# Attention scores by head in 32-row tiles, moved SBUF to SBUF into (column, head) rows, then mixed as one fp32 matmul a row pair; the low halves of the attention output on GpSimd

## The chip, the cores and the metric

The kernel runs on one core of one Trainium2 chip. The metric is the device time of one execution in microseconds (us). A core has five engines with a queue of instructions each: TensorE (PE, matmuls; PEld is its weight load), VectorE (DVE), ScalarE (ACT), GpSimd (POOL) and SyncE (SP, which here only issues DMAs). They run beside each other and wait for one another by semaphores. SBUF is the memory of 128 partitions that the engines read and write; PSUM holds the results of matmuls in 8 banks, which this kernel uses in four pairs: `psA`, `psL`, `psM`, `psC`.

## The reference

The input is 128 images of 384 channels and 14 x 14 = 196 pixels. After a group norm, a block of eight-head attention is added to it:

```python
q = conv1x1_bn(x, qw, ...)   # 8 heads x 32 channels, 196 pixels
k = conv1x1_bn(x, kw, ...)   # the same
v4 = conv1x1_bn(x, vw, ...)  # 8 heads x 128 channels
vl = depthwise 3x3 conv of v4, scaled and shifted
attn = jnp.einsum('bhid,bhjd->bhij', q, k) * SCALE
attn = attn + ab[:, BIAS_IDXS][None]
attn = jnp.einsum('bhij,gh->bgij', attn, th1w) + _c(th1b)
attn = jax.nn.softmax(attn, axis=-1)
attn = jnp.einsum('bhij,gh->bgij', attn, th2w) + _c(th2b)
o = jnp.einsum('bhij,bhjd->bhid', attn, v)
o = relu(o in channels first + vl)
return conv1x1_bn(o, pw, ...)    # x + this is the output
```

The heads are mixed twice: by `th1w` before the softmax and by `th2w` behind it.

## The kernel before

It works through 64 pairs of images, one pair in a round (`step(t, first, last)` on each engine; round 0 and the last one are written apart, the 62 between them are a loop). The order on each engine is the order in which its code is written; waits on counting semaphores tie the engines together.

A matmul of 32-bit data comes in two kinds here. A plain fp32 matmul is run by the chip as two instructions over the columns. The fp32r kind takes one instruction, but keeps fewer bits, so a product is made of three of them (`split3`, L293): high half by low half, low by high, high by high. The halves are made by a cast (ACT) and a subtraction.

TensorE's order in a round is this. Twelve projection tiles of 9 fp32r matmuls with 392 columns each (`qkv_tile`, both images side by side): value tiles 0 and 1, four tiles of queries and keys, value tiles 2 to 7. Then two of the three tiles of the output projection of the pair before (`project`, 24 matmuls each). Then the logits, already mixed by `th1w`: for each of 14 steps, two image rows `b` of queries (14 pixels by 8 mixed heads are 112 rows) by 196 keys, as 12 fp32r matmuls of 196 columns, since the mixing weight is multiplied into the queries, and all 8 heads' 256 channels are summed. The third projection tile follows; then 14 uses of the second mixing (`L404`, which also turns the attention into rows by key, against `mixw`); then `attn` by values (`L426`), eight units of one image and two heads (4 fp32 matmuls each, 196 columns).

The operands of the logits cost the other engines work: 16 scaled copies `q_hi` on ACT (`mixed_high`, L486), 16 `q_lo` on DVE (`mixed_low`, L722), two `k_hi` on ACT (L490), two `k_lo` on POOL (L857). DVE also does the depthwise convolution, 64 instructions a round (`conv`, L700), two block transposes of the values (L730), for each logit row the bias and the row's maximum (L759), the sum of attention and convolution (`s_add`, L794) and the low half `o_lo` of the relu's output (`low`, L787). ACT takes projection results out of PSUM, makes the exponentials (L584, 28 rows), copies the mixed attention out of PSUM (L601), puts the values into head order (`head_major`, L494) and applies the relu (`o_hi`, L461). POOL normalises the next pair (L822), makes `mixw` (L844), adds the residual (L833) and makes `x_lo` of the next pair (L827), for which TensorE's next round waits (`s_xlo`).

SP issues, in a round: the next pair's input; 8 DMAs of the transposed values to DRAM (L254); a row of ones; 4 DMAs that bring them back by key (L267); the store of the pair before; the residual's load.

## Time and profile before

| | |
|---|---|
| median of 3 runs | 4534.61 us (4534.28 to 4535.59) |
| profiled execution, its own time | 4534.58 us |
| its span, first to last instruction | 4532.8 us |
| granted TensorE clock over the span | 0.999 |
| busy: PE, DVE, ACT, POOL | 4505.5, 4197.4, 3570.3, 1360.9 us |
| share of PE in the chain that ended last | 99% |

The page divides the span by engine, by stretch of time and by group of instructions. The busy time of a group is the union of its instructions. The mean of one is longer than the distance between two starts, because an engine overlaps the end of one instruction with the next: a 392-column fp32r matmul has a mean of 341 to 345 ns, while 156 of them in a row take 27.85 us, 0.1785 us each. The distances are what fills an engine's time, so those are read from the timeline and from the chain in order of time.

### The profile page before, as it was taken

To read this page: it belongs to the slowest core of one execution; us is meant where nothing else is said; L and a number is where in the kernel's file an instruction comes from. 1 tells how busy PE (TensorE), PEld (TensorE's weight loads), DVE (VectorE), ACT (ScalarE), POOL (GpSimd) and SP (SyncE) were. 2 spreads that over 40 slices of the span, in tenths; PEclk is the share of its full clock that TensorE was granted. 3 is DMA by queue.
4 is the path that set the end of the run, shared out by engine and by line. 5 is a ranking of instruction groups with operands and counts; after the bars stand their busy time and mean duration, and the time that the engine had idled before them with its cause. 6 is when DMAs were issued, how large, how long until landed. Compare 5 with 4: busy or idle time off the path is not lost.

```text
span 4532.8 us, 108461 instructions
## 1 busy us (share of the span) xinstructions
PE 4505.5 (99%) x33666; PEld 4502.5 (99%) x33666; DVE 4197.4 (93%) x10015; ACT 3570.3 (79%) x8508; POOL 1360.9 (30%) x1288
## 2 busy tenths in 40 slices
PE   7999999999999999999999999999999999999999
PEld 7999999999999999999999999999999999999999
DVE  8999999999999999999999999999999999999998
ACT  7787877878778787787787877878778778787786
POOL 2323323323233232332322323323233232332322
PEclk9999999999999999999999999999999999999999
DMA  3322222223222232222322322223222232232222
GB/s 94 97 65 81 86 69 87 65 81 92 70 81 74 72 97 65 81 82 68 93 65 81 88 72 82 68 78 97 65 81 79 67 97 65 81 86 68 88 65 76
DMA packets 211502, 356.05 MB, mean 79 GB/s; under 512 B 15843, under 2 KB 132691, under 8 KB 211413
## 3 DMA queue, kind: packets, MB, share of 16 engines
q1 hardware_dynamic: 211478, 355.75, 27.3%
q8 instruction: 13, 0.21, 0.0%
q14 instruction: 11, 0.09, 0.0%
HBM read 199.71 MB, written 155.98 MB: 78 GB/s over the span
## 4 chain that ended last, share of the span: by engine, by line
PE 99%; DMA 0%; POOL 0%; DVE 0%; SPq 0%; ACT 0%; issue 0%; POOLq 0%; DVEq 0%
PE psA L293 45%; PE psA L426 15%; PE psL L293 13%; PE psM L293 10%; PE psM L404 9%; PE psL L404 7%; PE psA L306 0%; DMA qa<-in_wqkv 0%; SPq L254 0%; POOL xs L822 0%; DVE probs L730 0%; DMA by_key<-probs 0%; POOL wp_lo L863 0%; DVE q_lo L722 0%; ACT w_hi L443 0%
## 5 line engine op out<-in xcount | busy, mean ns | idle before, releaser
L700 DVE SCALAR_TENSOR_TENSOR psC<-vpad,par,psC 128x406 f32<-128x406 f32 x3072 | 1807.2, 635 | 0.0
L584 ACT ACTIVATE probs<-probs,nmax 112x196 f32<-112x196 f32 x1792 | 803.2, 451 | 128.8 <-DVE nmax L759 112.9
L293 PE MATMUL psA<-x_hi,w_lo 128*128 128x392 f32 x2304 | 794.9, 345 | 6.0 <-DVE x_lo L679 6.0
L293 PE MATMUL psA<-x_hi,w_hi 128*128 128x392 f32 x2304 | 785.7, 341 | 0.0
L293 PE MATMUL psA<-x_lo,w_hi 128*128 128x392 f32 x2304 | 785.1, 341 | 0.0
L426 PE MATMUL psA<-qa,shared 105*128 105x196 f32 x4096 | 690.9, 329 | 0.0
L426 PEld LDWEIGHTS psA<-qa,shared 105*128 105x128 f32 x4096 | 677.2, 190 | 0.4 <-DVE shared L794 0.3
L857 POOL TENSOR_TENSOR k_lo<-qk,k_hi 128x392 fp32r<-128x392 f32 x128 | 159.9, 1249 | 1636.4 <-ACT k_hi L490 1636.4
L722 DVE SCALAR_TENSOR_TENSOR q_lo<-qk,th,q_hi 128x392 fp32r<-128x392 f32 x1024 | 618.3, 632 | 2.0 <-ACT q_hi L486 1.9
L486 ACT ACTIVATE q_hi<-qk,th 128x392 fp32r<-128x392 f32 x1024 | 594.5, 618 | 2.1
L461 ACT ACTIVATE o_hi<-shared 128x392 fp32r<-128x392 f32 x512 | 271.6, 530 | 391.3 <-DVE shared L794 391.3
L293 PE MATMUL psL<-k_hi,q_lo 128*112 128x196 f32 x2048 | 534.4, 261 | 5.3 <-DVE q_lo L722 4.2
L293 PE MATMUL psL<-k_lo,q_hi 128*112 128x196 f32 x2048 | 536.2, 262 | 0.0
L293 PE MATMUL psL<-k_hi,q_hi 128*112 128x196 f32 x2048 | 535.9, 262 | 0.0
L293 PE MATMUL psA<-o_hi,wp_lo 128*128 128x392 f32 x1536 | 526.6, 343 | 0.0
L293 PE MATMUL psA<-o_lo,wp_hi 128*128 128x392 f32 x1536 | 523.1, 341 | 0.0
L293 PE MATMUL psA<-o_hi,wp_hi 128*128 128x392 f32 x1536 | 521.0, 339 | 0.0
L844 POOL TENSOR_TENSOR mixw<-kron,rinv 112x448 f32<-112x448 f32 (+1 forms) x512 | 455.9, 921 | 135.5 <-DVE rinv L773 123.3
L510 ACT ACTIVATE vpad<-psA,par 128x392 f32<-128x392 f32 x512 | 349.5, 683 | 141.6 <-PE psA L293 135.0
L700 DVE SCALAR_TENSOR_TENSOR psC<-vpad,par,shared 128x406 f32<-128x406 f32 x512 | 327.4, 661 | 143.0 <-ACT shared L456 143.0
L293 PEld LDWEIGHTS psA<-x_hi,w_lo 128*128 128x128 f32 x2304 | 434.3, 189 | 6.4 <-issue 6.4
L404 PE MATMUL psM<-mixw,probs 113*105 113x112 f32 x4096 | 435.9, 260 | 4.6 <-POOL mixw L844 4.6
(85 smaller groups left out, 10723.1 us busy)
## 6 DMA issues: line engine op xcount, KB each, us to landing
by_key<-probs SPq DMA_DIRECT2D x512, 224.0 KB, 3.6
qa<-by_key SPq DMA_DIRECT2D x128, 448.0 KB, 4.3
qk<-by_key SPq DMA_DIRECT2D x128, 448.0 KB, 6.9
xs<-in_x SPq DMA_DIRECT2D x64, 588.0 KB, 3.8
shared<-in_x SPq DMA_DIRECT2D x64, 588.0 KB, 3.8
out<-shared SPq DMA_DIRECT2D x63, 588.0 KB, 3.0
qa<-in_wqkv SPq DMA_DIRECT2D x3, 768.0 KB, 7.1
stage_wp<-in_wp SPq DMA_DIRECT2D x1, 1536.0 KB, 9.6
```

The costliest lines, as they stand in the source:

```text
L293: last = nc.tensor.matmul(dst, w, r, start=(begin and n == 0), stop=(end and n == 2))
L404: mm = nc.tensor.matmul(bank[:, jc, :, b, :], probs[0:HP + 1, img, 2 * n + b, jc * HALF:(jc + 1) * HALF], mixw[0:HP + 1, img, 2 * n + b, : ...
L426: mm = nc.tensor.matmul(psA[:, u % 2, e * PIX:(e + 1) * PIX], vt[0:HALF, img, jc, g * D:(g + 1) * D], attn[:, img, jc, g, :], start=(jc == ...
L461: nc.scalar.activation(o_hi[:, 2 * n:2 * n + 2, img * PIX:(img + 1) * PIX], acc[:, 2 * n:2 * n + 2, img * IMG:img * IMG + PIX], ACT.Relu). ...
L486: nc.scalar.activation(q_hi[dst], src, ACT.Copy, scale=th1[:, kt, g:g + 1]).then_inc(s_qhi, 1)
L510: nc.scalar.activation(dst[:, :, 0:RES, 0:RES], psA[:, m % 2, 0:COLS].rearrange("p (i r w) -> p i r w", i=2, w=RES), ACT.Identity, bias=qk ...
L584: nc.scalar.activation(row, row, ACT.Exp, bias=nmax[:, img, b:b + 1], scale=-1.0, accum_out=rowsum[:, img, b:b + 1]).then_inc(s_exp, 1)
L700: nc.vector.scalar_tensor_tensor(a if tap == 7 else sums, src, taps[:, c, TAPS[tap]:TAPS[tap] + 1], a if tap == 0 else sums, MUL, ADD).the ...
L722: nc.vector.scalar_tensor_tensor(q_lo[dst], src, th1[:, kt, g:g + 1], q_hi[dst].bitcast(f32), MUL, SUB).then_inc(s_qlo, 1)
L844: nc.gpsimd.tensor_tensor(mixw[0:HP, img, b0:b0 + nb, :], k2, rinv[:, img, b0:b0 + nb].unsqueeze(2).broadcast_to([HP, nb, HP]), MUL).then_ ...
L857: nc.gpsimd.tensor_tensor(k_lo[:, kt, :], k[:, kt, :], k_hi[:, kt, :].bitcast(f32), SUB).then_inc(s_klo, 1)
```

## The change

Scores are now made by head, before any mixing. `head_scores` comes behind each of value tiles 2 to 5: for one image and one part of the query pixels (8 of 14 columns `w`, or the other 6), 8 plain fp32 matmuls of 32 channels (one head) by 196 keys; four heads lie on four groups of 32 partitions and write four different PSUM banks. ACT and DVE copy the result to `scores` (two copies each). SP then moves each head's block with one DMA from `scores` (rows by query pixel) to `by_head`, whose row is (column `w`, head), with the image row `b` and the key along it: 8 DMAs a unit, 32 a round. Each has 112 or 84 runs of 784 bytes, and writes 8 or 6 partitions. The first mixing is now one plain fp32 matmul of 392 columns for each of the 14 steps, with `kron1` as weights. `q_hi`, `q_lo`, `k_hi` and `k_lo` are gone.

Around that: the three projection tiles of the pair before stand behind mixing matmuls 3, 7 and 11; the values are transposed by image, behind rows 3 and 7, and their way through DRAM follows the moves on SP's queue; the row of ones is loaded once; the units of `attn` by values go head pair by head pair with the two images in turn, and wait for all 14 copies of the mixed attention; ACT applies the relu twice (to `o_hi` and in place), POOL makes `o_lo` from the two (`low`); `x_high` of the next pair stands behind the first relu, and `x_low` behind POOL's first `low`; POOL takes over the head order of image 0's values.

```diff
+        heads_at = VT // 2 * ACC
+        by_head = shared[0:HP, heads_at:heads_at + 2 * RES * PIX].rearrange("p (i n) -> p i n", i=2)
...
+            def moves(t, u):
+                img, c = UNITS[u]
+                sp.wait_ge(s_score_a, 8 * t + 2 * u + 2)
+                sp.wait_ge(s_score_v, 8 * t + 2 * u + 2)
+                lo, hi = c * WIDE // RES, (c * WIDE + score_rows(c)) // RES
+                for h in range(NH):
+                    sp.dma_start(by_head[lo * NH + h:(hi - 1) * NH + h + 1:NH, img, :].rearrange("w (b j) -> w b j", b=RES),
+                                 scores[0:score_rows(c), img, c, h, :]).then_inc(s_moved[u], 16)
...
+            def head_scores(t, first, u):
+                img, c = UNITS[u]
+                if u:
+                    pe.wait_ge(s_score_a, 8 * t + 2 * u)
+                    pe.wait_ge(s_score_v, 8 * t + 2 * u)
...
+                at_ = img * PIX + c * WIDE
+                for kt in range(QT):
+                    for r in range(QUADS):
+                        part_ = slice(r * KD, (r + 1) * KD)
+                        mm = nc.tensor.matmul(score_bank(r)[0:score_rows(c), kt * PIX:(kt + 1) * PIX],
+                                              q[part_, kt, at_:at_ + score_rows(c)],
+                                              k[part_, kt, img * PIX:(img + 1) * PIX], start=True, stop=True)
+                mm.then_inc(s_score_mm, 1)
...
+                    if n % 7 == 0:
+                        pe.wait_ge(s_moved[2 * img], MOVES * (t + 1))
+                        pe.wait_ge(s_moved[2 * img + 1], MOVES * (t + 1))
...
-                            mm = split3(logit_bank(n)[:, (b - b0) * PIX:(b - b0 + 1) * PIX],
-                                        q_lo[:, img * RES + b, kt, :], q_hi[:, img * RES + b, kt, :],
-                                        k_lo[:, kt, px], k_hi[:, kt, px], kt == 0, kt == QT - 1)
-                    mm.then_inc(s_logit_mm, 1)
+                    nc.tensor.matmul(logit_bank(n)[:, 0:2 * PIX], kron1[:, :, :].rearrange("p g i -> p (g i)"),
+                                     by_head[:, img, b0 * PIX:(b0 + 2) * PIX], start=True, stop=True
+                                     ).then_inc(s_logit_mm, 1)
...
+                pe.wait_ge(s_mix_sb, 14 * t + 14)
+                for u in range(8):
+                    n, img = divmod(u, 2)
...
+                nc.scalar.activation(o_hi[:, 2 * n:2 * n + 2, img * PIX:(img + 1) * PIX], a, ACT.Relu).then_inc(s_relu, 1)
+                nc.scalar.activation(a, a, ACT.Relu).then_inc(s_relu, 1)
...
+                convs(13)
+                if first:
+                    dve.wait_ge(s_wlo, CT)
+                for u in range(4):
+                    score_copies(u)
+                    convs(2 if u < 3 else 3)
...
+                    if n in (3, 7):
+                        turn(n // 4)
+                        convs(2)
+                    if n == 11:
+                        convs(5)
...
-                convs(3)
-                convs(64)
+                convs(22)
...
+                nc.gpsimd.tensor_tensor(o_lo[sl], a, o_hi[sl].bitcast(f32), SUB).then_inc(s_olo, 1)
...
                 mixing_weights(t, first, 0)
+                head_major(t, 0)
+                head_major(t, 1)
                 mixing_weights(t, first, 1)
                 if not first:
                     residual(t, 2)
+                low(t, first, 0)
```

On TensorE in the loop, behind value tile 2 (`psA` is the projections' pair of banks), there stood before the next projection tile at once:

```order
L293 MATMUL psA<-x_hi,w_hi 128x392
L359 REGISTER_ALU
L293 MATMUL psA<-x_hi,w_lo 128x392 [waits s_qk_sb]
L293 MATMUL psA<-x_lo,w_hi 128x392
L293 MATMUL psA<-x_hi,w_hi 128x392
```

Now the first unit of scores stands between the two tiles (`qk_room` holds queries and keys):

```order
L309 MATMUL psA<-x_hi,w_hi 128x392
L358 REGISTER_ALU
L360 REGISTER_ALU [waits s_qk_sb]
L365 MATMUL psL<-qk_room 112x196 [waits s_mix_sb]
L365 MATMUL psL<-qk_room 112x196
L365 MATMUL psM<-qk_room 112x196 x2
L365 MATMUL psL<-qk_room 112x196 x2
L365 MATMUL psM<-qk_room 112x196 x2
L309 MATMUL psA<-x_hi,w_lo 128x392 [waits s_qk_sb]
```

Eight matmuls of the scores have come in between two tiles, four heads and then the other four.

On TensorE where the logits begin, there stood before, behind two whole projection tiles (`o_hi,wp_hi` is the last of them):

```order
L293 MATMUL psA<-o_hi,wp_hi 128x392
L369 REGISTER_ALU
L370 REGISTER_ALU [waits s_klo]
L376 ISA [waits s_qlo]
L293 MATMUL psL<-k_hi,q_lo 112x196 [waits s_mix_sb]
L293 MATMUL psL<-k_lo,q_hi 112x196
L293 MATMUL psL<-k_hi,q_hi 112x196
```

Now the first mixing matmuls stand directly behind the last value tile (`shared` holds `by_head`, `kron` is `kron1`), and the first projection tile behind the fourth of them:

```order
L309 MATMUL psA<-x_hi,w_hi 128x392
L406 REGISTER_ALU
L409 REGISTER_ALU [waits s_score_v,s_score_a]
L413 MATMUL psL<-shared,kron 112x392 [waits s_moved1,s_moved0]
L413 MATMUL psL<-shared,kron 112x392
L413 MATMUL psM<-shared,kron 112x392
L417 REGISTER_ALU
L418 REGISTER_ALU [waits s_v_sb]
L322 MATMUL psA<-mv,same 128x4 [waits s_stat]
L413 MATMUL psM<-shared,kron 112x392
```

The 48 projection matmuls that lay between the last value tile and the logits are gone from there, three logit steps of 12 matmuls each are three single ones, and the first of them waits for the DMAs of units 0 and 1.

On SP in the loop, behind the load of the next pair's input, there stood before:

```order
L225 DMA xs<-in_x 128x2x588
L251 ISA
L254 DMA by_key<-probs 32x7x256 [waits s_turned]
L254 DMA by_key<-probs 32x7x256 x7
L259 REGISTER_ALU
L260 DMA probs<-in_ones 1x3584 [waits s_vt_out]
L264 REGISTER_ALU
L267 DMA qa<-by_key 112x1024 [waits s_logit_mm]
```

Now 32 moves come first (`qa` holds `scores`, and later `turned`):

```order
L227 DMA xs<-in_x 128x2x588
L286 REGISTER_ALU
L261 REGISTER_ALU [waits s_olo,s_av_mm]
L265 DMA shared<-qa 8x14x196 [waits s_score_v,s_score_a]
L265 DMA shared<-qa 8x14x196 x7
L261 REGISTER_ALU
L265 DMA shared<-qa 6x14x196 [waits s_score_v,s_score_a]
L265 DMA shared<-qa 6x14x196 x7
L261 REGISTER_ALU
L265 DMA shared<-qa 8x14x196 [waits s_score_v,s_score_a]
L265 DMA shared<-qa 8x14x196 x7
L261 REGISTER_ALU
```

The transposed values' way out to DRAM stands behind all four units on this queue, and has the same 8 DMAs, four an image.

## Rows read from the trace of the kernel before

**Rows 1.** Page: the chain's shares by engine; granted clock in 40 slices.

```profile
PE 99%; DMA 0%; POOL 0%; DVE 0%; SPq 0%; ACT 0%; issue 0%; POOLq 0%; DVEq 0%
...
PEclk9999999999999999999999999999999999999999
```

**Rows 2.** Chain in order of time, one round: start us, us, what.

```profile
2056.45 27.85 PE psA L293 x156
2084.30 2.35 PE psL L293 x24
...
2101.03 4.31 PE psA L293 x24
2105.35 1.54 PE psM L404 x16
...
2114.55 1.53 PE psM L404 x16
2116.08 10.63 PE psA L426 x64
2126.71 0.18 PE psA L293
```

**Rows 3.** Busy time of that round: PE, PEld, DVE, ACT, POOL, then clock, DMA.

```profile
2056.45:2126.71 70.26, 70.26 (x527) 70.25 (x527) 65.39 (x156) 55.70 (x133) 21.21 (x20) 1.00 0.27 78
```

**Rows 4.** Groups by form: instructions that go, or move engine; busy us, mean ns.

```profile
L722 DVE SCALAR_TENSOR_TENSOR q_lo<-qk,th,q_hi 128x392 fp32r<-128x392 f32 x1024 | 618.3, 632 | 2.0 <-ACT q_hi L486 1.9
L486 ACT ACTIVATE q_hi<-qk,th 128x392 fp32r<-128x392 f32 x1024 | 594.5, 618 | 2.1
...
L787 DVE SCALAR_TENSOR_TENSOR o_lo<-shared,o_hi 128x392 fp32r<-128x392 f32 x512 | 285.6, 558 | 8.1
...
L827 POOL TENSOR_TENSOR x_lo<-xs,x_hi 128x1176 fp32r<-128x1176 f32 x63 | 169.7, 2694 | 255.1 <-ACT x_hi L439 255.1
L857 POOL TENSOR_TENSOR k_lo<-qk,k_hi 128x392 fp32r<-128x392 f32 x128 | 159.9, 1249 | 1636.4 <-ACT k_hi L490 1636.4
L494 ACT COPY shared<-qa 105x1024 f32<-105x1024 f32 x128 | 135.4, 1058 | 0.0
```

**Rows 5.** Timeline of ACT: copies out of PSUM, relu.

```profile
2108.30 0.97 ACT L601 COPY qa<-psL 105x448 f32<-105x448 f32 x2
...
2119.46 0.53 ACT L461 ACTIVATE o_hi<-shared 128x392 fp32r<-128x392 f32 x1 [0.44 <-DVE shared L794]
```

**Rows 6.** Timeline of DVE: convolutions, sum, low half.

```profile
2110.17 6.66 DVE L700 SCALAR_TENSOR_TENSOR psC<-vpad,par,psC 128x406 f32<-128x406 f32 x12
...
2118.86 0.57 DVE L794 TENSOR_TENSOR shared<-psA,shared 128x392 f32<-128x392 f32 x1 [0.46 <-PE psA L426]
2119.34 0.56 DVE L787 SCALAR_TENSOR_TENSOR o_lo<-shared,o_hi 128x392 fp32r<-128x392 f32 x1
```

**Rows 7.** Timeline of SP's DMA issues: start us, us.

```profile
2079.55 6.32 SPq L254 DMA_DIRECT2D by_key<-probs  x8
...
2101.07 0.79 SPq L267 DMA_DIRECT2D qa<-by_key  x2
```

**Rows 8.** DMA, 2079.5 to 2089.5 us, slices of 0.25 us; issue to landing.

```profile
GB/s 0 0 0 66 217 221 209 213 209 201 213 152 209 307 311 287 250 193 168 242 311 344 258 229 283 283 291 291 303 238 258 221 193 131 41 0 0 0 0 0
...
by_key<-probs SPq DMA_DIRECT2D x8, 224.0 KB, 3.5
```

**Rows 9.** DMA, 2115.6 to 2119 us: the load of the next pair's input.

```profile
GB/s 0 0 0 0 0 0 0 0 0 0 0 0 111 138 111 111 55 83 111 0 28 138 166 166 332 360 387 415 387 443 443 415 415 387 415 332 387 332 249 138
```

**Rows 10.** First round: busy times and clock, columns as in rows 3.

```profile
60.00:65.00 5.00, 0.96 (x10) 0.79 (x8) 5.00 (x23) 3.97 (x16) 5.00 (x3) 1.00 0.63 180
65.00:70.00 5.00, 4.49 (x29) 4.52 (x30) 5.00 (x11) 1.80 (x3) 5.00 (x7) 0.66 1.00 265
```

**Rows 11.** Chain in order of time, first round.

```profile
65.52 3.18 PE psM L404 x16
68.69 1.77 PE psL L404 x16
70.46 1.53 PE psM L404 x16
```

More of the change, by code:

```diff
@@ L71, in build @@
         same = sb("same", [P, P])
-        small = sb("small", [HP, 2 * NH + RES + 1])
+        small = sb("small", [HP, 2 * NH + 2 * RES + 1])
         mhalf = sb("mhalf", [P, 2])
@@ L87, in build @@
         proj = sb("proj", [P, CT, COLS])
-        k_hi = over("k_hi", [P, QT, COLS], QT * COLS)
-        k_lo = over("k_lo", [P, QT, COLS], 2 * QT * COLS)
-        qk = sb("qk", [P, 3, QT, COLS])
-        q_hi = over("q_hi", [P, 2 * RES, QT, HP])
+        qk_room = sb("qk_room", [P, 4 * COLS + 2 * RUN])
         qa = sb("qa", [P, 4 * RES * HP])
@@ L103, in build @@
         stage_wp = sb("stage_wp", [P, VT * COLS])
-        q_lo = over("q_lo", [P, 2 * RES, QT, HP], VT // 2 * ACC)
-        shared = sb("shared", [P, VT * ACC + 4 * DH + GAP + CT * COLS])
+        shared = sb("shared", [P, VT * ACC + 4 * DH + CT * COLS])
         psA = ctx.enter_context(nc.psum_tensor("psA", [P, 2, BANK], f32))
@@ L187, in group, with score_bank, score_rows @@
             return b // 4
-        def mixed(kt, g):
-            return ((slice(None), slice(None), kt, slice(g * RES, (g + 1) * RES)),
-                    q[:, kt, :].rearrange("p (b i) -> p b i", i=RES))
+        def score_bank(r):
+            return (psL if r < 2 else psM)[:, r % 2, 0:2 * PIX]
+        def score_rows(c):
+            return WIDE if c == 0 else REST
+        UNITS = [(img, c) for img in range(2) for c in range(2)]
         USES = [(img, n) for img in range(2) for n in range(7)]
@@ L387, in step @@
                         pe.wait_ge(s_stat, 4 * (t + 1))
                         group_sums(t + 1)
-                if not first:
-                    project(t, 2, True)
-                pe.wait_ge(s_ones_in, 16 * (t + 2))
+                    if n in (3, 7, 11) and not first:
+                        if n == 7 and not last:
+                            pe.wait_ge(s_gs, t + 2)
+                        project(t, n // 4, True)
+                if first:
+                    pe.wait_ge(s_ones_in, 16)
@@ L854, in step @@
             def step(t, first, last):
-                for kt in range(QT):
-                    wait_alone(pool, s_khi, 2 * t + kt + 1)
-                    nc.gpsimd.tensor_tensor(k_lo[:, kt, :], k[:, kt, :], k_hi[:, kt, :].bitcast(f32),
-                                            SUB).then_inc(s_klo, 1)
                 if first:
@@ L880, in step @@
                     x_low(t + 1)
+                for u in range(1, 8):
+                    low(t, first, u)
             rounds(pool, step)
```

387 lines of the change are left out of this document (180 added, 207 removed).

## The prediction

> **What bounds the kernel now.** I read the chain of work that ended last first: TensorE holds 99% of it, at a full granted clock throughout [rows 1]. The chain in order of time shows why: in a round of 70.26 us one stretch of matmuls follows the other without a gap [rows 2]. Twelve projection tiles and two output tiles, 156 matmuls, take 27.85 us (0.1785 each, so 1.61 a tile); the logits run from 2084.30 to 2101.03, 16.73; the third output tile 4.31; seven pairs of mixing uses 1.53 each, 10.74 in all; attention by values 10.63 for eight units, 1.33 a unit. The busy times of the same round say how near the others are: DVE 65.4, ACT 55.7, POOL 21.2 [rows 3]. So TensorE work taken away comes off the time, until a wait stands in its place. Outside its 64 rounds the execution has 4532.8 - 64 x 70.26 = 36 us.
>
> **What goes and what comes on TensorE.** The 168 fp32r matmuls of the logits go: 16.7 us. The mixing matmuls come: two instructions over 392 columns each. Attention by values is of that kind, 64 instructions of 196 columns in 10.63 us [rows 2], 0.166 each; twice the columns, 0.33; so 0.66 a step and 9.3 us for 14, with the group sum. The scores come: 4 units x 8 matmuls x 2 instructions of 196 columns. One after the other they are 16 x 0.166 = 2.66 us a unit, 10.6 a round. No row shows two matmuls side by side in the array, so I bound the unit by 2.66 and by a quarter of it, 0.66. I take 1.5: the two instructions of one matmul use the same 32 rows and follow each other, but the next head's first can run beside this one's second, which is nine instruction times, 9 x 0.166. Then the sum is -16.7 + 9.3 + 6.0 = -1.4 us a round (-4.8 with 0.66, +3.2 with 2.66), if nothing waits.
>
> **The other engines' account.** DVE loses 16 `q_lo` at about 0.55 and 8 `o_lo` at about 0.49, and gets 8 copies at about 0.48 (the `s_add` sum also reads PSUM and starts 0.48 before its follower) [rows 4, 6]: about -9 us. ACT loses 16 `q_hi` (594.5 / 1024 = 0.58 at most), two casts and two of its four 1.06 us head copies, and gets 8 copies (0.49 each by L601) and 8 relus of 0.53 [rows 4, 5]: about -4 us. POOL loses two `k_lo` of 1.25 and gets 8 low halves of about the same size (1.1 each) and two head copies, which I bound by ACT's 1.06 and by the rate of `x_lo`, 2.69 for 1176 columns, so 2.35 for 1024 [rows 4]: about +10 us. None of them comes near the round's length. Their sums cost nothing; their places in the chain do.
>
> **The moves.** Each is 112 x 784 bytes, 88 KB (84 x 784, 66 KB, for the 6-column part), and writes 8 (6) partitions. The price has these bounds. Below: SP's issue, 0.40 us [rows 7] (two take 0.79). Above: the 8 value DMAs read 32 partitions each and ran at 201 to 221 GB/s at first [rows 8], where the input load over 128 partitions reaches 415 to 443 [rows 9]. So the rate falls with the partitions reached. If it fell all the way in proportion, 8 partitions would give 55 GB/s and 1.6 us a move. I take the step between: 220 GB/s over 16 DMA engines is 13.7 each; if each destination partition is served by one engine, 8 engines give 110 GB/s, 0.80 us, and 6 engines with 66 KB again 0.80. That is nearest to rows 8, since it is the same engine rate, and a run of 784 bytes is near their 1024. The Trainium skill (SBUF — State Buffer, "Door 1: The DMA port swizzle") says that bandwidth depends on how many of the 16 ports the partitions reach, 27.2 GB/s a port, and that partition p + 32 shares p's port. By it 32 partitions give 218 GB/s, with which rows 8 agree, and the partitions h, h+8, ... of a move reach four ports, 109 GB/s, 0.81 us. The sum does not need it.
>
> **The round, step by step** (us from its first tile). Seven tiles: 11.25. First unit to 12.75. Two copies each on ACT and DVE with their ends, 1.3: SP starts at 14.1. The queue is then full: the later units' copies are ready every 3.1 us, eight moves take 6.4. Sixteen moves end at 14.1 + 12.8 = 26.9, and land 2.1 later (issue to landing is 3.5 at a service of 1 to 1.4 [rows 8]): 29.0. TensorE is ready at 12 x 1.61 + 4 x 1.5 = 25.3. **It waits 3.7 us ahead of the first mixing matmul.** Seven mixing steps, the group sum and one output tile, 9.2: step 7 is due at 38.2. Units 2 and 3 have landed at 14.1 + 25.6 + 2.1 = 41.8. **It waits 3.6 us again.** Steps 7 to 13 with two output tiles, 13.2: 55.0. Here ACT must end its exponentials before it copies mixed rows, 0.5 wait; second mixing 10.7; then attention by values needs the 14th copy: 0.8. 67.1. DVE behind the last row: three convolutions, the reciprocal, 22 convolutions at 0.555 [rows 6] and the first sum, 15.1 us after 55.0, while TensorE could start its third unit 14.7 after it: about 0.7 with the signals. 10.6 of attention: 78.4. The last sums and ACT's second relu hold the next round's first tile by 0.4. `x_high` and `x_low` end before that: 70.1 + 1.0 + 1.2 + 2.7 = 75.0. **A round of 78.8 us.** In short: 70.3 - 1.4 + 3.7 + 3.6 + 0.5 + 0.8 + 0.7 + 0.4 = 78.6, rounding apart.
>
> The values' way through DRAM is now behind 25.6 us of moves; image 0's are back at about 55, its head copies on POOL end by 60, `mixw` of image 1 begins at 60.8, and TensorE reaches use 7 at 60.9. That is even; each us more there is a us on the round, if POOL's copies cost more than 2.35.
>
> **The clock.** In the first round TensorE was busy 0.96 of 5 us, and the 5 us behind it had a granted clock of 0.66: part of it at the lower level, 1.2 GHz, instead of 2.4 [rows 10]. The mixing stretches then took 3.18 and 1.77 instead of 1.53: 1.9 us lost [rows 11]. Two waits of 3.6 us a round may do the same. The first loss is free, since the second wait shrinks by it; of the second I count half, 0.9. That makes 79.7 a round, and 64 x 79.7 + 36 = **5137 us**. The span and the run's own time differ by 1.8 us, and the median of the runs is 4534.61, so the same number stands for it.
>
> **The rivals.**
>
> (a) *Moves hidden.* If a move costs 0.5 or less, both waits vanish: unit 1 has landed at 14.1 + 8 + 2.1 = 24.2, units 2 and 3 at 32.2 where 34.5 is due. The round is 78.8 - 7.3 = 71.5 with units of 1.5, 76 with 2.66: 4610 to 4900 us. For it: packets are only a little smaller than in rows 8, and SBUF to SBUF needs no DRAM. Against it: 8 partitions are a quarter of those in rows 8.
>
> (b) *Faster.* Moves as in (a) and four heads truly side by side, 0.8 us a unit: 71.5 - 2.8 = 68.7, 64 x 68.7 + 36 = 4430 us. It decides below 0.5 us a move and below 1.2 a unit. The Trainium skill (TensorE: Matmul & The Clock Gate, "Part 3: Packing small matmuls — row/col tiling") says that matmuls on different row groups run concurrently, 3.07 times as fast for four; by that alone a unit is 2.66 / 3.07 = 0.87 us, and with moves at 0.80 the round still ends at 78, since it starts the moves only 0.6 us earlier.
>
> (c) *Row tiles that don't overlap.* The change then doesn't do what it says: 2.66 a unit. SP starts at 15.3, the round is 80.0 with moves at 0.80. It lies within the forecast.
>
> (d) *The rate falls in proportion to partitions*, 1.6 us a move: 32 x 0.8 = 25.6 more: 104 a round, 6720 us. For it: nothing but the halving from 128 to 32. Against it: that halving is a factor of 2 for 4.
>
> **How the numbers follow.** Forecast, moves at 0.70 to 1.0, with (c) in it: 75.6 to 86 a round, 4870 to 5540 us; chance 0.60. (a) 0.17. (b) 0.15. (d) 0.05. 0.03 for something between (a) and (b) that ends at no change. The range of 8 in 10 leaves out (d), the upper end of the forecast's and most of (b): 4560 to 5450. A measurement here tells a difference of 0.2% (9 us). Faster by more: 0.15; within: 0.03; slower: 0.82.
>
> **What would show it.** In the profile after, the first mixing matmul (L413, step 0) and step 7 wait for DMAs `shared<-qa`, 3 to 4 us each; the DMA view from 14 to 40 us of a round shows about 110 GB/s; TensorE's share of the chain drops to about 90%, the DMAs of the moves hold the rest; the granted clock shows less than 1. If step 0 does not wait, (a) is right, and the distance between two tiles around a unit of scores (1.5, 0.7 or 2.7 us) tells (b) from the rest. My forecast falls if moves run beside each other faster than 13.7 GB/s an engine, or if POOL's head copies hold use 7 for longer than the moves do.

## The result, and the profile after

The changed kernel takes 5164.18 us (median of 4 runs, 5140.64 to 5175.93), the kernel before 4535.10 us beside it. The ratio is 1.138, with a 95% interval of 1.134 to 1.142: slower by 14%. The prediction was 5137 us, in a range of 4560 to 5450, with a chance of 0.82 for slower: right in time and direction.

The page of the changed kernel, its profiled execution (5171.08 us): span, busy times, granted clock in 40 slices, and the chain of work that ended last by engine and by line.

```profile
span 5169.1 us, 101484 instructions
PE 4597.6 (89%) x28802; PEld 4009.0 (78%) x28802; DVE 3712.8 (72%) x8992; ACT 3333.0 (64%) x8252; POOL 1782.9 (34%) x1800
...
PEclk9999999999999999999999999999999999999999
...
PE 49%; SPq 20%; issue 14%; DVE 10%; DMA 7%; DVEq 1%; ACT 0%; ACTq 0%; POOLq 0%
PE psA L309 28%; SPq L265 19%; PE psA L459 9%; DMA shared<-qa 6%; DVE psC L723 5%; PE psL L413 5%; PE psM L413 4%; DVE shared L799 1%; DVE shared L723 1%; DVE probs L766 1%; PE psL L365 1%; DVE qa L739 1%; PE psM L437 1%; PE psL L437 0%; DV
```

In [rows 1] TensorE held 99% of the chain. Now it holds 49%. SP's queue holds 20%, nearly all of it line 265, the moves, and the DMAs of the moves another 6%. Over half of DVE's 10% (L723), and much of the issue time between its instructions, are its late convolutions. The forecast had said that TensorE's share would drop to about 90%. That sign was misread: by the forecast's own steps the path of a round lies in SP's queue from 14.1 to 29.0 us, and later in DVE's convolutions, and while it lies there TensorE's work is not on it.

The waits of TensorE over the whole span: engine, line, what it waited for, us in total, times, longest. The idle time in these rows and in brackets counts from the modelled end of the instruction before, which is later than the point from which the next could have started, so a stall seen by the starts is up to 0.3 us longer.

```profile
PE psL L413 <- DMA shared<-qa: 327.0, 64, 5.7
...
PE psA L459 <- DVE shared L799: 74.2, 63, 1.9
...
PE psM L413 <- DMA shared<-qa: 49.0, 34, 2.2
...
PE psA L459 <- ACT qa L623: 40.0, 64, 0.7
...
PE psM L437 <- ACT qa L623: 24.0, 64, 1.8
```

Step 0 waits for the moves in each of the 64 rounds, 5.1 us in the mean. Step 7 waits for them in 34, 1.4 us each, 0.8 a round. The third unit of attention by values waits for DVE's first sum, 1.2 us a round; the first unit waits for ACT's 14th copy, 0.6; one use of the second mixing waits 0.4.

One round, from its first tile at 2509.38 to the next at 2588.09: 78.7 us where [rows 3] had 70.26. It is one of the shorter ones: the mean is (5169.1 - 36) / 64 = 80.2 us, with the prediction's 36 us outside the rounds. TensorE's timeline: start, us, instruction, and in brackets the idle time before it.

```profile
2538.49 2.93 PE L413 MATMUL psL<-shared,kron 112*112 112x392 f32 x4 [5.27 <-DMA shared<-qa]
...
2548.59 1.48 PE L413 MATMUL psL<-shared,kron 112*112 112x392 f32 x4
...
2550.93 0.91 PE L413 MATMUL psM<-shared,kron 112*112 112x392 f32 x2 [0.20 <-DVE nmax L766]
...
2579.54 8.23 PE L459 MATMUL psA<-qa,shared 105*128 105x196 f32 x48 [0.33 <-DVE shared L799]
2588.09 0.44 PE L309 MATMUL psA<-x_hi,w_lo 128*128 128x392 f32 x1 [0.32 <-DVE shared L799]
```

Step 0 comes 29.1 us behind the first tile (it was forecast for 29.0). A score unit between two tiles, TensorE's timeline again:

```profile
2520.64 0.34 PE L309 MATMUL psA<-x_hi,w_hi 128*128 128x392 f32 x1
2520.91 0.42 PE L365 MATMUL psL<-qk_room 32*112 32x196 f32 x2
...
2521.51 0.33 PE L365 MATMUL psM<-qk_room 32*112 32x196 f32 x2
2521.77 0.45 PE L309 MATMUL psA<-x_hi,w_lo 128*128 128x392 f32 x1
```

From the start of the last matmul of one tile, 2520.64 and 0.18 long, to the first of the next, 2521.77, is 0.95 us. In it lie eight matmuls of two instructions each; the instructions for `psL` and `psM` start 0.01 us apart. The sixteen start in four groups of four, so four heads run side by side.

SP's timeline of the same round: the 32 moves take 23.0 us to issue, 0.72 each, and the eight value DMAs of line 254 come behind them (in [rows 7] they had the queue to themselves).

```profile
2523.05 23.02 SPq L265 DMA_DIRECT2D shared<-qa  x32
2547.21 9.93 SPq L254 DMA_DIRECT2D by_key<-qa  x8
```

Busy times by stretch, columns as in [rows 3]: the 5 us in which step 0 arrives, the 10 behind them, and the whole round.

```profile
2535.00:2540.00 5.00, 1.51 (x3) 0.85 (x4) 0.00 (x0) 0.00 (x0) 0.00 (x0) 0.76 0.50 106
2540.00:2545.00 5.00, 5.00 (x13) 2.99 (x12) 2.38 (x15) 3.16 (x14) 1.32 (x5) 0.56 0.48 99
2545.00:2550.00 5.00, 5.00 (x27) 4.38 (x26) 3.70 (x8) 1.69 (x6) 4.96 (x3) 1.00 0.61 134
...
2509.40:2588.10 78.70, 71.61 (x451) 62.19 (x451) 56.98 (x141) 52.06 (x130) 27.50 (x29) 0.96 0.41 101
```

The granted clock falls to 0.76 and 0.56 around the end of the wait, so the lower level, 1.2 GHz, held for about 7 of these 10 us (0.24 and 0.44 are missing, and at half speed each counts double); the first four instructions of step 0 take 2.93 us together, where the same four take 1.48 at full clock (2548.59 above). The Trainium skill (TensorE: Matmul & The Clock Gate, "Part 1: The HAM clock gate (the \"warmup\" mystery)") describes these two levels, and a clock that falls for an idle TensorE; the rows agree. DVE (56.98 where it was 65.39) and ACT (52.06 for 55.70) have less to do than before, by 8.4 and 3.6 us where about 9 and 4 were reckoned; POOL has 6.3 more (27.50 for 21.21), where 10 were reckoned.

### The profile page after: what moved, and what is told of

It is laid out like the page before. It is cut to its first block, busy times and chain, and to the rows that moved or that the text cites. A ratio compares the mean times of both kernels' runs of the same rounds, so it can differ in the third digit from the quotient of the medians.

```text
span 5169.1 us, 101484 instructions
## 1 busy us (share of the span) xinstructions
PE 4597.6 (89%) x28802; PEld 4009.0 (78%) x28802; DVE 3712.8 (72%) x8992; ACT 3333.0 (64%) x8252; POOL 1782.9 (34%) x1800
## 4 chain that ended last, share of the span: by engine, by line
PE 49%; SPq 20%; issue 14%; DVE 10%; DMA 7%; DVEq 1%; ACT 0%; ACTq 0%; POOLq 0%
PE psA L309 28%; SPq L265 19%; PE psA L459 9%; DMA shared<-qa 6%; DVE psC L723 5%; PE psL L413 5%; PE psM L413 4%; DVE shared L799 1%; DVE shared L723 1%; DVE probs L766 1%; PE psL L365 1%; DVE qa L739 1%; PE psM L437 1%; PE psL L437 0%; DVE nmax L766 0%
## 5 line engine op out<-in xcount | busy, mean ns | idle before, releaser
L723 DVE SCALAR_TENSOR_TENSOR psC<-vpad,par,psC 128x406 f32<-128x406 f32 x3072 | 1758.8, 634 | 0.0
L766 DVE CUSTOM_DVE_ANT_0 probs<-psL,bias 112x196 f32<-112x196 f32 x1024 | 329.4, 360 | 793.4 <-PE psL L413 792.2
L459 PE MATMUL psA<-qa,shared 105*128 105x196 f32 x4096 | 738.2, 340 | 114.2 <-DVE shared L799 74.2
L413 PE MATMUL psL<-shared,kron 112*112 112x392 f32 x1024 | 471.9, 591 | 327.0 <-DMA shared<-qa 327.0
L847 POOL TENSOR_TENSOR o_lo<-shared,o_hi 128x392 fp32r<-128x392 f32 x512 | 475.4, 954 | 614.9 <-ACT shared L499 604.8
L309 PE MATMUL psA<-o_hi,wp_lo 128*128 128x392 f32 x1536 | 598.4, 390 | 0.3 <-DVE shared L799 0.3
L723 DVE SCALAR_TENSOR_TENSOR psC<-vpad,par,shared 128x406 f32<-128x406 f32 x512 | 378.1, 760 | 288.8 <-ACT shared L491 286.7
L413 PEld LDWEIGHTS psL<-shared,kron 112*112 112x112 f32 x1024 | 202.9, 206 | 451.7 <-issue 449.9
L437 PEld LDWEIGHTS psM<-mixw,probs 113*105 113x105 f32 x4096 | 416.4, 171 | 59.1 <-ACT qa L623 35.6
L866 POOL TENSOR_TENSOR mixw<-kron,rinv 112x448 f32<-112x448 f32 (+1 forms) x512 | 414.9, 841 | 101.8 <-DVE rinv L781 71.6
```

Of the source, the lines that this page charges most:

```text
L309: last = nc.tensor.matmul(dst, w, r, start=(begin and n == 0), stop=(end and n == 2))
L413: nc.tensor.matmul(logit_bank(n)[:, 0:2 * PIX], kron1[:, :, :].rearrange("p g i -> p (g i)"), by_head[:, img, b0 * PIX:(b0 + 2) * PIX], st ...
L437: mm = nc.tensor.matmul(bank[:, jc, :, b, :], probs[0:HP + 1, img, 2 * n + b, jc * HALF:(jc + 1) * HALF], mixw[0:HP + 1, img, 2 * n + b, : ...
L459: mm = nc.tensor.matmul(psA[:, u % 2, e * PIX:(e + 1) * PIX], vt[0:HALF, img, jc, g * D:(g + 1) * D], attn[:, img, jc, g, :], start=(jc == ...
L723: nc.vector.scalar_tensor_tensor(a if tap == 7 else sums, src, taps[:, c, TAPS[tap]:TAPS[tap] + 1], a if tap == 0 else sums, MUL, ADD).the ...
L766: nc.vector.tensor_tensor_reduce(out=keys(img, b), in0=logit_bank(n)[:, (r % 2) * PIX:(r % 2 + 1) * PIX].rearrange("p (r w) -> p r w", w=RES),
```

## The experiments

**1. Where the destination rows lie.** The forecast had 0.80 us a move from eight DMA engines at 13.7 GB/s, and the Trainium skill's ports gave the same number. Three kernels keep bytes, packets and count, and change only the place or the order.

```diff
-  sp.dma_start(by_head[lo * NH + h:(hi - 1) * NH + h + 1:NH, img, :]...
+  sp.dma_start(by_head[h * RES + lo:h * RES + hi, img, :]...
```

(head-rows; `small` and `abx` are laid out to match)

> Rows of by_head in order (head, column): a move writes 8 (6) neighbouring partitions and not every 8th; bytes, packets and the number of DMA engines that could serve it stay. Theory P (place): a move goes at the pace of the ways into SBUF that its destination partitions share, four neighbours to a way, 27 GB/s each; the changed kernel's moves reach four ways, these two or three. 1.2 to 1.6 us a move, 32 of them instead of 0.83: a round of 89 to 103 us instead of 79 to 80, 5730 to 6630 us in all. Theory N (number): 13.7 GB/s for each destination partition wherever it lies: 0.83 us a move, 5164 us within 0.5%.

```diff
+  row = c * QT * BLK + (h // QUADS) * QUADS * (hi - lo) + h % QUADS
-  sp.dma_start(by_head[lo * NH + h:(hi - 1) * NH + h + 1:NH, img, :]...
+  sp.dma_start(by_head[row:row + QUADS * (hi - lo - 1) + 1:QUADS, img, :]...
```

> Rows of by_head in an order in which a move writes every 4th partition. Theory P: eight (six) ways instead of four, 0.4 us a move by their pace, so that SP's issue of 0.59 to 0.76 us sets it. Units 0 and 1 have landed at 13.7 + 16 x 0.62 + 2.1 = 25.7 us of a round where TensorE is ready at 23.7: 2 us of wait instead of 5.3; units 2 and 3 at 36: none at step 7. A round of 72 to 75 us, 4640 to 4840 us. Theory N: nothing changes, 5164 us within 0.5%. A third possibility is that SP's issue alone (0.6 to 0.76 in the changed kernel) is the limit there too: then nothing changes either, and e1 stays at 5164.

```diff
-                for h in range(NH):
+                for h in (0, 4, 1, 5, 2, 6, 3, 7):
```

> The eight moves of a unit in the order of heads 0, 4, 1, 5, 2, 6, 3, 7, rows as in the changed kernel. Theory P: neighbours in the queue use different ways (partitions h, h+8, ... against h+4, h+12, ...), so two moves run abreast and the issue sets the pace, 0.62 to 0.7 us: 4640 to 4840 us as with every 4th partition. If a queue finishes one move before the next, nothing changes. Theory N: nothing changes, 5164 us within 0.5%.

Measured: neighbouring partitions 5247.5 us (ratio 1.157, 1.155 to 1.159), every 4th partition 5050.8 (1.1135, 1.112 to 1.115), the other order 4995.7 (1.1015, 1.099 to 1.104). The wait of step 0 in the three kernels, in this order:

```profile
PE psL L413 <- DMA shared<-qa: 480.1, 64, 7.9
```

```profile
PE psL L414 <- DMA shared<-qa: 256.2, 64, 4.2
```

```profile
PE psL L413 <- DMA shared<-qa: 218.3, 64, 3.6
```

The forecasts of theory P for the last two, 4640 to 4840 us, and for the first, 5730 to 6630, were both missed. The start of step 0 in e1:

```profile
2568.42 2.92 PE L413 MATMUL psL<-shared,kron 112*112 112x392 f32 x4 [7.51 <-DMA shared<-qa]
```

Theory N is dead: the same engines and bytes give 7.5, 4.0 and 3.4 us of wait a round, where the changed kernel has 5.1. Theory P has the right signs and wrong sizes. It wanted 1.2 to 1.6 us a move for neighbours; the 16 moves of image 0 were there 17.7 us behind their first issue (2550.75 to 2568.42), against 15.4 in the changed kernel, 14.4 with every 4th partition and 13.5 in the other order. So place and order are worth 4.2 us between the worst and the best, and something else sets the rest. Ten us of busy times out of the moves, first of the changed kernel, then of e1 and e3 (the last two columns are the DMA share and GB/s):

```profile
2526.00:2536.00 10.00, 7.22 (x61) 5.90 (x59) 5.59 (x11) 7.14 (x16) 0.00 (x0) 1.00 0.48 99
```

```profile
2553.70:2563.70 10.00, 7.21 (x61) 5.90 (x59) 5.58 (x11) 7.14 (x16) 0.00 (x0) 1.00 0.52 81
```

```profile
2510.50:2520.50 10.00, 7.24 (x61) 5.90 (x59) 5.62 (x11) 7.17 (x16) 0.00 (x0) 1.00 0.37 105
```

In the changed kernel the packets' time is 0.48 of what 16 DMA engines have, which is about eight engines all the time: they have a backlog. With neighbouring partitions it is 0.52, for only 81 GB/s. The Trainium skill (DMA: Bandwidth & Descriptors, "Why a DMA increments its semaphore by 16 and not by 1") says that a DMA is split over the largest number of engines, up to 16, that divides the slowest dimension of both sides, here 8 and 6; the rows fit it, but the share is no exact count of engines, as the 0.52 shows. In the other order the share is lower by a quarter (0.37) and more is moved, 105 GB/s for 99: each packet takes less time, and the engines wait for work. Both kernels issue 32 moves in the same 23.02 us.

**2. Issue or bytes?** SP's issue was the forecast's lower bound, 0.40 us by line 267. Here is line 265 in the changed kernel, least, middle and longest in ns, and in the kernel of experiment 4, which issues one move a unit, so that no other move stands ahead of it:

```profile
L265 SPq DMA_DIRECT2D shared<-qa x2048: 588/718/813, 30.2 to 5108.8; - x187
```

```profile
L265 SPq DMA_DIRECT2D shared<-qa x256: 620/730/867, 31.4 to 4507.9; - x128
```

Also without others around it a move takes SP 0.62 to 0.87 us. So the 0.72 is not a wait for the moves ahead. Half the bytes with as many packets:

```diff
-  by_head[...].rearrange("w (b j) -> w b j", b=RES),
-  scores[0:score_rows(c), img, c, h, :]
+  by_head[...].rearrange("w (b j) -> w b j", b=RES)[:, :, 0:PIX // 2],
+  scores[0:score_rows(c), img, c, h, 0:PIX // 2]
```

(half of each mixed row is stale, so this computes something else)

> The changed kernel with moves that carry 98 of 196 elements of each run: as many DMAs and packets, half the bytes; the other half of the mixed rows is stale, so this computes something else. Theory I (issue): SP needs 0.59 to 0.81 us to issue one move (0.72 in the mean, 23.0 us for 32, the same with one move a unit as with eight), and that sets the pace as soon as the packets are not slower; units 0 and 1 have landed at 13.7 + 10.7 + 2.8 = 27.2 us of a round as with the heads in the order 0, 4, 1, 5, ...: about 4996 us, 4950 to 5030. Theory B (bytes and DMA engines set the pace): half the time for each move, 0.4 us, both waits vanish, 4580 to 4700 us.

Measured, with the heads in the plain order: 4969.8 us (1.096, 1.094 to 1.098), 3.8% under the changed kernel and 0.5% under the other order with all bytes. Its wait at step 0, and ten us out of its moves:

```profile
PE psL L413 <- DMA shared<-qa: 188.2, 64, 3.0
```

```profile
2500.60:2510.60 10.00, 7.17 (x61) 5.90 (x59) 5.54 (x11) 7.12 (x15) 0.00 (x0) 1.00 0.22 50
```

Halving the bytes takes the backlog away, as the other order does, and then bytes no longer count: 50 GB/s and 0.22 of the engines, and step 0 still waits 2.9 us a round. The 32 moves take SP 23.0 us as before. Theory I holds. With the issue shared:

```diff
+  ACT_HEADS = {0: (3, 7), 1: (3, 7)}
-  for h in range(NH):                         # SP
+  for h in [h for h in (0, 4, 1, 5, 2, 6, 3, 7) if h not in ACT_HEADS.get(u, ())]:
...
   score_copy(t, u, 1)                         # ACT
+  if u in ACT_HEADS:
+      moves(act, t, u, ACT_HEADS[u])
```

(ACT's four `stat` go behind `values(7)`; ACT now waits for the copies of a unit before it issues)

> Heads in the order 0, 4, 1, 5, 2, 6, 3, 7 (4996 us by itself); ACT issues two of the eight moves of units 0 and 1, its four statistics of the next pair go behind the last value copy in exchange. Bytes, packets and DMA engines stay. Theory I: SP issues 12 moves and not 16 before step 0, units 0 and 1 have landed at 13.7 + 12 x 0.67 + 2.8 = 24.5 us of a round where TensorE is ready at 23.7: 0.8 us of wait instead of 3.4, the wait at step 7 is gone: 4996 - 64 x (2.6 + 0.4) = 4800 us, 4770 to 4860. If ACT's own issues (1.4 us in each of two intervals of 2.65 between score units) hold TensorE's tiles up as long as they save, it stays at 4990 to 5050. Theory B: nothing changes at step 0, 4996.

Measured: 4826.7 us (1.064, 1.062 to 1.066), inside the 4770 to 4860 expected, 3.4% under the other order by itself. The waits for moves at step 7 (`psM`) and at step 0 (`psL`), and what ACT's issues took in one round:

```profile
PE psM L415 <- DMA shared<-qa: 95.6, 61, 2.1
...
PE psL L415 <- DMA shared<-qa: 74.6, 64, 1.6
```

```profile
2498.33 1.32 ACTq L231 DMA_DIRECT2D shared<-qa  x2
...
2501.33 1.67 ACTq L231 DMA_DIRECT2D shared<-qa  x2
```

Step 0 waits 1.2 us a round and not 3.4, since SP issues 12 moves ahead of it and not 16. ACT pays 0.66 and 0.84 us a move in its own queue, and TensorE waits for it a little in the score units. Step 7 waits more often (61 times, 1.6 each), as step 0 comes earlier and the moves of units 2 and 3 still go through SP: what is won at the first wait is lost in part at the second, which was expected to go. Sharing the issue with GpSimd, which has the most idle time, was not tried.

**3. Does a DMA of twice the size halve the issues?**

```diff
-  UNITS = [(img, c) for img in range(2) for c in range(2)]
+  UNITS = [(img, c) for c in range(2) for img in range(2)]
-  sp.dma_start(by_head[rows, img, :].rearrange("w (b j) -> w b j", b=RES), scores[0:score_rows(c), img, c, h, :])
+  sp.dma_start(by_head[rows, :, :, :].rearrange("w b i j -> w (b i) j"), scores[0:score_rows(c), :, c, h, :])
```

(`by_head` now runs (column of the row tile, image, key); convolution centres and POOL's head copies wait for later steps)

> One DMA moves one head of both images (224 packets of 784 bytes, 16 DMAs a round and not 32); the score units go in the order image 0 and 1 of the first part, then of the second, so that the first move can start only behind the second unit (16.4 us of a round) and both images' rows land together. What does SP's issue cost by? Theory D (per DMA): 0.72 us each, two moves' packets then need 1.06 us at 8 DMA engines by the 38 ns an undisturbed packet takes (224 / 8 x 0.038), so the engines set the pace: first part landed by 16.4 + 8.5, second by 33.4 + 2: wait of 12 us at step 0, none at step 7: a round of 84, 5400 us. Theory K (per packet, 0.72 / 98 = 7.3 ns each): 1.44 us an issue, 16.4 + 16 x 1.44 + 3 = 42.5: wait of 19 us, none at step 7: a round of 90 us, 5800 us. The issue time in the profile decides, the total only follows it.

Measured: 6184.3 us (1.364), over both expectations. The issue times, SP's issues and step 0 of one round:

```profile
L265 SPq DMA_DIRECT2D shared<-qa x1024: 597/1201/2322, 33.4 to 6109.0; - x171
```

```profile
2527.80 20.26 SPq L265 DMA_DIRECT2D shared<-qa  x16
```

```profile
2558.14 2.93 PE L413 MATMUL psL<-shared,kron 112*112 112x392 f32 x4 [22.82 <-DMA shared<-qa]
```

Sixteen issues take 20.3 us, 1.27 each in the mean, 1.20 in the middle, where a move of half the packets takes 0.72. That looks like a price by packet (theory K, 1.44), but the single issues of this round say otherwise. SP's part of the chain in order of time, the first six:

```profile
2527.80 0.69 SPq L265
...
2528.54 0.61 SPq L265
...
2529.19 0.61 SPq L265
...
2529.84 0.60 SPq L265
...
2530.48 1.13 SPq L265
...
2531.65 1.20 SPq L265
```

The first four, with 224 packets each, take as long as the first four of the changed kernel with 112 (0.69, 0.61, 0.59 and 0.59 in the round above), and so they do in the middle of all 64 rounds. Only behind them do issues stretch, to 1.98 us in this round. So twice the packets cost nothing at the issue while little is queued (theory D, 0.72), and the later issues are held up. That it is the filled queue that holds them is likely and was not tested. Both forecasts of the total were too low, because the transfers fell behind the issues: the last rows are there 30.3 us behind the first issue, 10 behind the last. That is 1.9 us for one of these DMAs, or 0.95 for as many packets as one move has, near the 0.97 of e1 and over SP's 0.72. Fewer and larger DMAs can't help while the transfers themselves, heads in the plain order, need more than the issues.

What sets the 0.6 to 0.77 us of a move's issue is open, and a DMA's form alone doesn't tell it. The value DMAs of [rows 7] have 224 packets and 0.79 in the mean, but single ones take 0.33 to 1.13 us:

```profile
L254 SPq DMA_DIRECT2D by_key<-probs x512: 332/744/1127, 44.8 to 4474.0; - x171
```

**4. What is left without the moves' wait.**

```diff
-                for h in range(NH):
+                for h in range(1):
```

(seven of eight heads' rows are not moved and are stale, so this computes something else)

> Only head 0 of each unit is moved; the mixing matmuls read stale rows for the other heads, so this computes something else. It prices the wait for moves. If the moves are the whole cause: no wait at steps 0 and 7, TensorE loses 5.3 + 1.5 us of waiting and about 1 us by the lower clock behind it, a round of 70 to 72 us, 4520 to 4650 us. If DVE's chain of convolutions behind the last logits row or the values' way through DRAM takes their place, it stays over 75 us a round, 4840 us and more.

Measured: 4581.0 us (1.010, 1.008 to 1.012). Its span and busy times, and its granted clock:

```profile
span 4574.2 us, 99694 instructions
PE 4388.8 (96%) x28802; PEld 3920.0 (86%) x28802; DVE 3715.9 (81%) x8992; ACT 3303.4 (72%) x8252; POOL 1792.4 (39%) x1802
```

```profile
core 0: 4574.2 us, clock 0.995
```

So seven of eight moves cost (5169.1 - 4574.2) / 64 = 9.3 us a round. The waits of step 0 and 7 are 5.9 of them. Most of the other 3.4 is the lower clock: its mean is 0.951 in the changed kernel and 0.995 here, 0.044 x 80 = 3.5 us at most, since some of it falls into the wait itself, where it costs nothing; and TensorE is busy (4597.6 - 4388.8) / 64 = 3.3 us longer with the same 28802 instructions.

Where in the round the time goes is seen from the starts of TensorE's instructions. Means of 55 rounds in the middle of each execution, in us:

| stretch | changed kernel | one head (e4) | other order (e3) | and early convolutions (e7) |
|---|---|---|---|---|
| first tile to step 0 | 28.90 | 23.62 | 27.20 | 27.18 |
| step 0 to step 7 | 12.69 | 9.12 | 11.74 | 11.86 |
| step 7 to second mixing | 13.51 | 13.16 | 13.43 | 13.45 |
| second mixing to attention by values | 12.12 | 12.12 | 12.12 | 12.12 |
| attention to the next first tile | 13.04 | 12.99 | 12.95 | 11.20 |
| round | 80.26 | 71.02 | 77.45 | 75.81 |

From step 0 to step 7 the changed kernel takes 3.6 us more than e4: 0.8 of waiting at step 7, and 2.8 of slower work. But it is the landing that sets step 7: the last semaphore update of units 2 and 3 comes at 41.36 us of a round in the mean, and step 7 starts 0.22 to 0.37 us behind it in every one of the 55 rounds, also where the row of waits names none. SP's 32 issues take 23.0 us at either clock, so at full clock TensorE would only have waited there longer. So by itself the lower clock costs little in this kernel, an estimate of 0.4 us a round from the third row (13.51 - 13.16); it takes the place of a wait.

And with no wait for a move at all the kernel is still 1% slower than before. The chain there goes through DVE's convolutions behind the last row of logits. Eight of them moved forward, first in the kernel with all moves:

```diff
-  convs(2 if u < 3 else 3)
+  convs(2 if u < 3 else 11)
...
-  convs(22)
+  convs(14)
```

(the heads in the other order, as in e3)

> Heads in the order 0, 4, 1, 5, 2, 6, 3, 7 (4996 us by itself) and eight of DVE's convolutions moved from behind the last reciprocal to ahead of step 0, where DVE is idle for 5 us. DVE's chain behind the last row then ends 4.4 us earlier; TensorE's stall at its third unit of attention by values (L459 waits for the sum L799, 1.2 us a round, 76.6 us in all) is gone: 4996 - 77 = 4919 us, 4890 to 4940. Rival: the late chain is not what TensorE waits for, or DVE's eight convolutions end after step 0 has landed and delay the rows by as much: 4980 to 5010 us.

Measured: 4885.1 us (1.0775, 1.076 to 1.079), 2.2% under the same kernel without it (e3), a little more than the 1.5% expected. The 64 instructions of attention by values now run in one piece (2576.29 and 2579.54 were the starts of two pieces in the changed kernel):

```profile
2501.15 10.88 PE L459 MATMUL psA<-qa,shared 105*128 105x196 f32 x64 [0.62 <-ACT qa L623]
```

The gain is (4995.5 - 4883.3) / 64 = 1.75 us a round, and it lies in the last stretch of the table, 12.95 to 11.20. That is more than the 1.2 us of the row of waits, which counts too little at each stall: in the round above the third unit starts 3.25 us behind the first where 16 instructions need 2.66, a stall of 0.59 that the bracket has at 0.33. So DVE's late chain costs 1.8 us a round. The same two lines in the kernel with one move:

> One head moved per unit (4581 us by itself, the other heads' rows stale, so this computes something else) and eight convolutions ahead of step 0. It shows what the changed arithmetic is worth where no move holds it and DVE's late chain is gone (76.7 us of stall at the third unit of attention; 111 us came of it in the kernel with all moves): 4470 to 4510 us, below the kernel before. Rival: with no wait at step 0 the eight convolutions have no idle time to lie in and delay the first rows by 3 us: 4570 us or more.

Measured: 4470.0 us (0.986, 0.984 to 0.9875). With one move a unit and DVE's chain out of the way the changed arithmetic is worth 1.4% against the kernel before; the change as it was built had both in its way.

**5. All that helps.** The other order, ACT's share with two moves of unit 3 too, and nine convolutions earlier.

```diff
+  ACT_HEADS = {0: (3, 7), 1: (3, 7), 3: (3, 7)}
-  convs(2 if u < 3 else 3)
+  convs(2 if u < 3 else 7)
...
-  convs(2)                      # behind steps 3 and 7
+  convs(4 if n == 3 else 5)
...
-  convs(22)
+  convs(13)
```

> All that helped together: heads in the order 0, 4, 1, 5, 2, 6, 3, 7; ACT issues two moves each of units 0 and 1 and, behind its statistics, of unit 3; nine convolutions earlier (four more ahead of step 0, two more behind step 3, three more behind step 7). From ACT's share alone (4827 us): the wait at step 7 goes (95.6 us in all), DVE's stall at the third unit of attention goes (73.3 us): 4660 us, 4620 to 4720. It stays over the kernel before by what is left: 1.2 us of wait a round at step 0 and 0.4 by ACT. Rival: the more convolutions ahead of step 0 or ACT's two later moves delay the rows and the exponentials, and give back the half: 4720 to 4780 us.

Measured: 4632.5 us (1.021, 1.020 to 1.023), 10.3% under the changed kernel, as expected or a little better, and 2.1% over the kernel before.

```profile
PE psL L415 <- DMA shared<-qa: 80.9, 64, 1.7
```

Step 7 waits for moves in 8 rounds only, 3.3 us in all, and the clock is granted to 0.999, but 1.3 us at step 0 stay. No version here that moves all heads beats the kernel before.

**6. Are row tiles bound to the order of the heads?**

```diff
-                for kt in range(QT):
-                    for r in range(QUADS):
+                for r in range(QUADS):
+                    for kt in range(QT):
```

> The changed kernel with the eight matmuls of a score unit in another order: the two heads that use the same 32 rows of the array follow each other. Theory R: a matmul starts beside its forerunner only on other rows, and waits in the queue behind one on its own; then a unit takes 13 instruction times of 0.166, 2.2 us, and not 0.95 (two rows' heads in each case wait): each unit 1.2 us longer, SP starts 1.2 us later, TensorE is ready 4.8 later, of which most fills its wait: a round of 80.5 to 82, 5210 to 5320 us. Theory Q: matmuls on free rows may pass those that wait: 0.95 us a unit, 5164 us within 0.5%.

Measured: 5150.6 us (1.136, 1.1335 to 1.138), like the changed kernel's 5164.2 within the spread of its runs. A unit between two tiles:

```profile
2512.51 0.34 PE L309 MATMUL psA<-x_hi,w_hi 128*128 128x392 f32 x1
2512.78 0.43 PE L365 MATMUL psL<-qk_room 32*112 32x196 f32 x2
2512.81 0.43 PE L365 MATMUL psM<-qk_room 32*112 32x196 f32 x2
...
2513.40 0.34 PE L365 MATMUL psM<-qk_room 32*112 32x196 f32 x2
2513.66 0.45 PE L309 MATMUL psA<-x_hi,w_lo 128*128 128x392 f32 x1
```

The distance from 2512.51 + 0.18 to 2513.66 is 0.97 us, 0.95 before. Matmuls on the same 32 rows may follow each other in the program; the other rows are still filled at once.
## Why the prediction was right

Total, direction and mechanism came as forecast: TensorE waits for the moves at step 0, and the gain in arithmetic doesn't pay for it. Also the course of the round was met: step 0 at 28.9 us in the mean (forecast 29.0), step 7 at 41.6 (41.8), attention by values at 67.2 (67.1). Some of the terms behind it were wrong and cancelled, and the last stretch was luck. By its own steps:

- **TensorE's sum, -1.4 us.** A score unit was taken at 1.5 us between 0.66 and 2.66, and measures 0.95. The sum is -16.7 + 9.3 + 3.8 = -3.6, near what rival (b) had. The 1.5 let each head start one instruction behind the one before it; the trace has four heads starting together. This term changed the total little, since TensorE is ready earlier only to wait longer for step 0.
- **0.80 us a move.** The number holds: 16 moves were there 15.4 us behind the first issue, less the 2.1 us of landing that the forecast used, 0.83 each. The reason holds only in part. It took the DMA engines as the limit; but SP needs 0.72 for each issue, whatever the bytes, and destination rows that collide add the rest. The step that failed is the lower bound: 0.40 us was read from line 267 in [rows 7], two plain DMAs. The row above it, line 254, has many short runs as the moves have, and 6.32 / 8 = 0.79 in the mean. It too would have been an uncertain guide, as its single issues take 0.33 to 1.13, but it was a reason to doubt rivals (a) and (b), 0.32 of the chances and both resting on 0.5 us a move.
- **The Trainium skill's ports.** They gave 0.81 for this placement, which is near the 0.83, and 1.2 to 1.6 for e1, where 0.97 was measured ((17.7 - 2.1) / 16). That the place matters is shown; the rate by the number of ports reached is not.
- **3.7 us at step 0** are 5.1. Landing was met to 0.1 us; TensorE was ready 1.5 us sooner, since the units are shorter by 2.2 in all.
- **3.6 us at step 7** are 0.8. Step 7 was due at 38.2 and came at 41.6, the time of landing, since the lower clock stretches the steps before it by 2.8 us. The prediction said that the first loss would be free because the second wait shrinks by it, and so it was: 0.8 + 2.8 is the 3.6 forecast.
- **0.9 us for the clock** was meant for the second loss, behind step 7. There about 0.4 came.
- **0.8 and 0.5 around mixing** were met: by the starts 2576.29 - (2573.97 + 1.53) = 0.79 and 2567.76 - (2565.71 + 1.53) = 0.52; the rows of waits, which count less, have 0.6 and 0.4.
- **0.7 us for DVE's chain** is 1.8, by experiment 4. This term was mis-sized most: attention by values with the next tile's wait was forecast at 0.7 + 10.6 + 0.4 = 11.7 us and takes 13.0. That the clock was reckoned 0.5 too high makes up for part of it, so the 79.7 us a round that came so near to 80.2 are in part luck.
- **POOL's head copies**, bounded by 1.06 and 2.35, take 1.21, and in the loop no mixing use waited for POOL: the even race at use 7 was won.
- **The signs.** The DMA view showed 99 GB/s where about 110 were named. The two waits and the lower clock were there; the wait at step 7 was smaller, for the reason above, and TensorE's share of the chain was 49% and not 90%.

The rivals: (a) and (b) needed 0.5 us a move, and (b) units under 1.2, which is what the measured 0.95 is. Experiment e4 comes nearest to these conditions, and gives 4581 us, not the 4430 of (b): DVE's chain, the 0.95 for 0.8, and the clock account for most of the difference (1.1, 0.6 and about 0.3 us a round). So this change as built would have been no gain even with the moves hidden. Only e9, which also moves the convolutions, gets to 4470. (c) fell with the 0.95 us. (d), 1.6 us a move, was not reached even with neighbouring partitions.

## What to carry to other kernels

Before many small DMAs replace arithmetic, multiply their count by the issue time of a DMA of the same form: a move took SP 0.6 to 0.8 us here whatever the bytes, and 32 of them were 23 us of an 80 us round. Look at single issues and not at their mean: a mean can hide that the first ones are cheap and the later ones are held up. If the queue sets the pace, spread the issues over two queues and let neighbours in the queue write to different partitions, before changing sizes. And where TensorE waits for some us in each round, expect a lower clock behind the wait, 3 us of slower work a round here; but count it only where no later wait would have taken up the time anyway. Here one did, and about 0.4 us was left.

## What the runs showed that was not expected

- A move's issue took SP 0.59 to 0.69 us with 8 destination partitions (112 packets) and 0.72 to 0.77 with 6 (84 packets), by the middle of each place in the round: fewer packets, more time. With neighbouring or every 4th partition 32 took 24.3 us, 6% more.
- The order of the heads alone, no byte or engine changed, was worth 3.3% (5164 to 4996 us).
- Twice the packets in a DMA cost nothing at the issue for the first four of a round (0.69, 0.61, 0.60, 0.60 us); the later ones stretched up to threefold.
- Half of the bytes of all moves, in the plain order, gave 4970 us, about what the order alone gave with all bytes (4996). What halving gives with the order changed as well was not tried.
- A wait of 5 us was followed by 2.8 us of slower work that cost nothing, since the next wait shrank by as much.
- Eight matmuls on 32-row tiles ran four abreast in either order: 0.95 us for 16 instructions of 196 columns, which one after the other are 2.66 by [rows 2].
